# Router logits of a gated cross-attention and expert kernel: made transposed in four column groups of TensorE and turned back by a second product

## The reference

```python
x = x + tanh(g_xattn) * xattn(layernorm(x), ctx, ctx, mask, Wq, Wk, Wv, Wo, bo)
xf = layernorm(x).reshape(-1, 256)
logits = xf @ Wg + bg                      # [1024, 8], the router
idx = argmax(softmax(logits), axis=-1)     # one expert for each token
h = gelu(einsum('th,ehi->tei', xf, W1) + b1)
y = einsum('tei,eih->teh', h, W2) + b2
x = x + tanh(g_ffn) * y[t, idx[t]]
```

## Time and profile before

| What | us |
|---|---|
| median of the runs | 199.1 (lowest 198.98) |
| profiled execution | 200.14 |
| its span on the core | 198.3 |
| TensorE busy in the span | 185.5 |
| VectorE busy | 123.5 |
| ScalarE busy | 104.9 |
| GpSimd busy | 89.5 |

### The profile page before, as it was taken

One profiled execution on the slowest core, in us unless ns is written; L12 is line 12 of the kernel. 1 busy time (PEld: TensorE's weight loads), 2 busy tenths in 40 slices (PEclk: granted clock), 3 DMA queues, 4 the chain that ended last, 5 costly groups with the idle time before them and its releaser, 6 DMA issues.

```text
span 198.3 us, 4265 instructions
## 1 busy us (share of the span) xinstructions
PE 185.5 (94%) x1412; PEld 136.2 (69%) x1412; DVE 123.5 (62%) x538; ACT 104.9 (53%) x376; POOL 89.5 (45%) x128
## 2 busy tenths in 40 slices
PE   7999999999899999999999899998999999999960
PEld 6994455666665444788895666765788899989940
DVE  3479576899996421154459999997833556355520
ACT  3243438899998112211427899997631263445410
POOL 6000002577778991000003899768810024776650
PEclk9999999999999999999999999999999999999996
DMA  4998008999999990480000101600000002353011
GB/s 134 335 369 284 0 3 265 319 287 315 298 317 266 206 326 20 146 279 1 0 2 3 55 27 54 198 0 0 3 0 2 0 3 76 110 153 109 34 53 31
DMA packets 22323, 25.19 MB, mean 127 GB/s; under 512 B 1987, under 2 KB 20877, under 8 KB 22160
## 3 DMA queue, kind: packets, MB, share of 16 engines
q1 hardware_dynamic: 19536, 21.83, 37.3%
q0 software_dynamic: 1152, 2.12, 3.2%
q10 hardware_dynamic: 1600, 0.84, 1.5%
HBM read 14.14 MB, written 11.68 MB: 130 GB/s over the span
## 4 chain that ended last, share of the span: by engine, by line
PE 69%; DVE 21%; issue 3%; ACT 2%; POOL 1%; POOLq 1%; DVEq 0%
PE s_bank L1729 14%; PE o_bank L1674 14%; DVE probs L1308 12%; PE s_bank L2035 8%; PE o_bank L2046 7%; PE s_bank L1769 5%; DVE oT L1335 4%; PE s_bank L1608 3%; PE s_bank L1639 2%; PE o_bank L1817 2%; PE o_bank L1799 2%; PE t_bank L1700 2%; PE s_bank L1844 2%; ACT probs L832 2%; PE s_bank L2024 1%
## 5 line engine op out<-in xcount | busy, mean ns | idle before, releaser
L649 POOL TENSOR_TENSOR probs<-probs,r_col 128x512 f32<-128x512 f32 x32 | 33.3, 1040 | 73.8 <-DVE r_col L1319 73.7
L832 ACT ACTIVATE probs<-probs,negm_run 128x160 f32<-128x160 f32 x128 | 53.0, 415 | 6.1 <-DVE negm_run L1308 5.9
L1308 DVE CUSTOM_DVE_ANT_0 probs<-s_bank,maskneg 128x160 f32<-128x160 f32 x128 | 33.3, 317 | 3.5 <-PE s_bank L1769 3.2
L1729 PE MATMUL s_bank<-xnT,wq_sb 128*128 128x512 f32 x64 | 29.0, 600 | 0.0
L1674 PE MATMUL o_bank<-wo_sb,oT 128*128 128x256 f32 x128 | 28.7, 380 | 0.0
L1674 PEld LDWEIGHTS o_bank<-wo_sb,oT 128*128 128x128 f32 x128 | 23.9, 190 | 3.5 <-issue 0.5
L832 ACT ACTIVATION_READ_ACCUMULATOR probs<-probs,negm_run 128x1 f32 x128 | 23.9, 187 | 0.0
L1769 PE MATMUL s_bank<-k_sb,q_sb 64*128 64x160 f32 x256 | 21.7, 306 | 0.0
L1729 PEld LDWEIGHTS s_bank<-xnT,wq_sb 128*128 128x128 f32 x64 | 11.7, 190 | 13.1 <-issue 12.8
L628 POOL DMA_INDIRECT out_dram<-oT x16 | 17.0, 1064 | 7.8 <-DVE oT L1256 5.9
L1769 PEld LDWEIGHTS s_bank<-k_sb,q_sb 64*128 64x128 f32 x256 | 18.0, 187 | 2.7 <-DVE negm_run L1308 1.5
(11 more groups left out here) (169 smaller groups left out, 299.6 us busy)
## 6 DMA issues: line engine op xcount, KB each, us to landing
sorted_rows<-empty_row SPq DMA_DIRECT2D x8, 1040.0 KB, 15.6
oT<-in_L_ffn_W_dram SPq DMA_DIRECT2D x1, 2048.0 KB, 18.2
q_sb<-in_L_ffn_W_dram SPq DMA_DIRECT2D x1, 2048.0 KB, 9.4
oT<-sorted_rows SPq DMA_DIRECT2D x1, 1040.0 KB, 5.2
oT<-sorted_rows SPq DMA_DIRECT2D x8, 130.0 KB, 2.3
wq_sb<-in_L_xattn_Wq_dram SPq DMA_DIRECT2D x2, 512.0 KB, 8.1
mask_sb<-in_mask_BxSxS_bk_dram SPq DMA_DIRECT2D x2, 512.0 KB, 8.9
wv_sb<-in_L_xattn_Wv_dram SPq DMA_DIRECT2D x1, 1024.0 KB, 10.8
```

Source lines behind the costliest of these rows:

```text
L649: nc.gpsimd.tensor_tensor(window_wide(u), window_wide(u), r.rearrange("p i h -> p (i h)") .unsqueeze(2).broadcast_to([P, 4, WIDE]), ALU.mu ...
L832: last = nc.scalar.activation(window_part(u, i, h), window_part(u, i, h), ACT.Exp, bias=negm_run[at], scale=-1.0, accum_out=l_run[at])
L1308: nc.vector.tensor_tensor_reduce(window_part(u, i, h), s_bank[u % 2][:, h, i * CK:i * CK + WK], maskneg[:, q, 0:WK], -SCALE, LARGEST, ALU. ...
L1729: last = nc.tensor.matmul(bank[m % 4], wq_sb[:, c, m * P:(m + 1) * P], xnT[:, c, b * N:(b + 1) * N], start=(c == 0), stop=(c == DC - 1))
```

## The change

The weights are padded: `wg_sb` becomes [128, 2, 32] and `bg_sb` [128, 32] (`LEFT_E` = 32), zeroed by GpSimd, with 8 of the 32 columns loaded; ScalarE waits for the zeros before it issues the two loads. Now `wg_sb` is the stationary operand and the transposed tile the moving one, so a product gives logits transposed: 32 partitions (8 used) by 128 tokens. The four groups of 32 partitions of one PSUM bank hold four such products.

- Batch 0 (`batch_logits`): one group for each of the four tiles, with a bias product and two products over the contraction halves each. It is called once, after the second key product; the transposes of tile 3 move from there to after the first. VectorE copies the 128 x 128 result to `logitT` (`take_logitT`), and after the third key product TensorE transposes it back (`batch_logits_back`).
- Batch 1 (`half_logits`): two tiles per route and two contraction halves in four groups, without adding the halves. VectorE copies, and a product with `fold` (two 64 x 64 identities one over the other, made by GpSimd at the start of the attention) adds the halves and turns them back (`half_logits_back`). For route 1 the two calls stand before the projection of tile 7, with one pair of chunk transposes between them; for route 2 after the result of expert 0, with the chunk transposes of expert 4, which move up, between them.
- VectorE's `take_logitT(r)` stands at the head of `route_logits(r)` for routes 1 and 2, and after a key copy (`k1`) for route 0. `logit_ps` now counts twice per route.

The diff, cut:

```diff
+    LEFT_E = P // QT
...
+        wg_sb = sb("wg_sb", [P, DC, LEFT_E])
+        bg_sb = sb("bg_sb", [P, LEFT_E])
+        logitT = sb("logitT", [P, P])
+        fold = sb("fold", [P, DH])
...
-                sp.wait_ge(empty_ready, 2)
+                sp.wait_ge(empty_ready, 4)
...
+            nc.gpsimd.memset(wg_sb[:], 0.0).then_inc(empty_ready, 1)
+            nc.gpsimd.memset(bg_sb[:], 0.0).then_inc(empty_ready, 1)
...
             def normalise_window(b, also):
+                if b == 0:
+                    pool.wait_ge(ident_ready, E + 3)
+                    nc.gpsimd.tensor_tensor(fold[:], ident[:, 0:DH], ident[:, DH:P], ALU.add).then_inc(fold_ready, 1)
+                    pool.wait_ge(fold_ready, 1)
...
+            act.wait_ge(empty_ready, 2)
+            act.dma_start(bg_sb[:, 0:E], bg.unsqueeze(0).broadcast_to([P, E])).then_inc(s_small, 16)
+            act.dma_start(wg_sb[:, :, 0:E], wg.rearrange("(c p) e -> p c e", p=P)).then_inc(s_small, 16)
...
+            def take_logitT(r):
+                dve.wait_ge(logit_ps, 2 * r + 1)
+                nc.vector.tensor_copy(logitT[:], bank[5][:, P:2 * P]).then_inc(logitT_taken, 1)
             def route_logits(r):
...
+                logits = bank[5][:, 2 * P:2 * P + tiles * LEFT_E].rearrange("p (t e) -> p t e", e=LEFT_E)[:, :, 0:E]
+                if r > 0:
+                    take_logitT(r)
+                dve.wait_ge(logit_ps, 2 * r + 2)
...
                 if where == "k1":
+                    take_logitT(0)
                     route_logits(0)
...
+            def half_logits(r):
+                at = ROUTED[r][0]
+                pe.wait_ge(xt2_sb, at + 2)
+                part = [bank[5][g * LEFT_E:(g + 1) * LEFT_E, P:2 * P] for g in range(4)]
+                for t in range(2):
+                    nc.tensor.matmul(part[t], bg_sb[0:1, :], ones[0:1, :], start=True, stop=False)
+                for k in range(DC // 2):
+                    for g in range(4):
+                        c = g // 2 * (DC // 2) + k
+                        tt = at + g % 2
+                        last = nc.tensor.matmul(part[g], wg_sb[:, c, :], xnT[:, c, tt * P:(tt + 1) * P],
+                                                start=(g >= 2 and k == 0), stop=(k == DC // 2 - 1))
+                last.then_inc(logit_ps, 1)
+            def half_logits_back(r):
+                pe.wait_ge(logitT_taken, r + 1)
+                nc.tensor.matmul(bank[5][:, 2 * P:2 * P + 2 * LEFT_E], logitT[:], fold[:], start=True, stop=True)\
+                    .then_inc(logit_ps, 1)
+            def batch_logits():
+                pe.wait_ge(xt2_sb, QT)
+                by_tile = [bank[5][t * LEFT_E:(t + 1) * LEFT_E, P:2 * P] for t in range(QT)]
+                for t in range(QT):
+                    nc.tensor.matmul(by_tile[t], bg_sb[0:1, :], ones[0:1, :], start=True, stop=False)
                 for c in range(DC):
+                    for t in range(QT):
+                        last = nc.tensor.matmul(by_tile[t], wg_sb[:, c, :], xnT[:, c, t * P:(t + 1) * P], start=False,
+                                                stop=(c == DC - 1))
+                last.then_inc(logit_ps, 1)
+            def batch_logits_back():
+                pe.wait_ge(logitT_taken, 1)
+                nc.tensor.transpose(bank[5][:, 2 * P:3 * P], logitT[:], ident[:]).then_inc(logit_ps, 1)
...
                 if where == "k1":
-                    tile_logits(2)
+                    xn2_transposes(3)
                 elif where == "k2":
-                    xn2_transposes(3)
+                    batch_logits()
                 elif where == "k3":
-                    tile_logits(3)
+                    batch_logits_back()
...
                         project_tile(2)
-                        tile_logits(0)
                         xn2_transposes(1)
...
-                        tile_logits(1)
                         xn2_transposes(2)
...
                 xn2_transposes(QT + 1)
-                tile_logits(QT)
                 chunk_transposes(0, 2)
+                half_logits(1)
                 chunk_transposes(0, 3)
-                tile_logits(QT + 1)
+                half_logits_back(1)
                 project_tile(QT + 3)
                 ranks(1)
                 xn2_transposes(QT + 2)
                 hidden(0, 2)
-                pe.wait_ge(rank_taken, 4)
-                tile_logits(QT + 2)
                 xn2_transposes(QT + 3)
...
                 result(0, 0, expert_w2(0))
-                tile_logits(QT + 3)
+                pe.wait_ge(rank_taken, 4)
+                half_logits(2)
+                chunk_transposes(0, 4)
+                half_logits_back(2)
                 hidden(0, 3)
                 result(0, 1, expert_w2(1))
                 ranks(2)
-                chunk_transposes(0, 4)
                 result(0, 2, expert_w2(2))
```

More of the change, by code:

```diff
@@ L151, in flamingo_kernel @@
         b2_sb = sb("b2_sb", [P, E, D])
-        wg_sb = sb("wg_sb", [P, DC, E])
-        bg_sb = sb("bg_sb", [P, E])
+        wg_sb = sb("wg_sb", [P, DC, LEFT_E])
+        bg_sb = sb("bg_sb", [P, LEFT_E])
+        logitT = sb("logitT", [P, P])
         bo_sb = sb("bo_sb", [P, D])
@@ L274, in flamingo_kernel @@
         ident_ready = sem("ident_ready")
+        fold_ready = sem("fold_ready")
         pool_step = sem("pool_step")
@@ L314, in flamingo_kernel @@
         logit_ps = sem("logit_ps")
+        logitT_taken = sem("logitT_taken")
         count_ready = sem("count_ready")
@@ L783, in _ @@
             act.dma_start(bo_sb[:], bo.unsqueeze(0).broadcast_to([P, D])).then_inc(s_small, 16)
-            act.dma_start(bg_sb[:], bg.unsqueeze(0).broadcast_to([P, E])).then_inc(s_small, 16)
-            act.dma_start(wg_sb[:], wg.rearrange("(c p) e -> p c e", p=P)).then_inc(s_small, 16)
+            act.wait_ge(empty_ready, 2)
+            act.dma_start(bg_sb[:, 0:E], bg.unsqueeze(0).broadcast_to([P, E])).then_inc(s_small, 16)
+            act.dma_start(wg_sb[:, :, 0:E], wg.rearrange("(c p) e -> p c e", p=P)).then_inc(s_small, 16)
             done = act.alloc_register("act_done")
@@ L1150, in _ @@
             left = dve.alloc_register("dve_left")
+            def take_logitT(r):
+                dve.wait_ge(logit_ps, 2 * r + 1)
+                nc.vector.tensor_copy(logitT[:], bank[5][:, P:2 * P]).then_inc(logitT_taken, 1)
             def route_logits(r):
                 R = routes[r]
-                at, tiles = ROUTED[r][0] % QT, ROUTED[r][1]
+                tiles = ROUTED[r][1]
                 shape = [P, tiles, E]
-                logits = bank[5][:, at * E:(at + tiles) * E].rearrange("p (t e) -> p t e", e=E)
-                dve.wait_ge(logit_ps, r + 1)
+                logits = bank[5][:, 2 * P:2 * P + tiles * LEFT_E].rearrange("p (t e) -> p t e", e=LEFT_E)[:, :, 0:E]
+                if r > 0:
+                    take_logitT(r)
+                dve.wait_ge(logit_ps, 2 * r + 2)
                 then(nc.vector.tensor_reduce(R.lmax[:], logits, AX.X, ALU.max))
@@ L1400, in attend @@
                     nc.vector.tensor_copy(*k_dst(u + 1)).then_inc(S.k_dve, 1)
+                    also(f"k{u}")
                 dve.wait_ge(S.mask_ready, n + 1)
@@ L1442, in route_first_batch @@
             def route_first_batch(where):
-                if where == "k":
+                if where == "k1":
+                    take_logitT(0)
+                elif where == "k":
                     route_logits(0)
@@ L1686, in xn2_transposes @@
                 last.then_inc(xt2_ps, 1)
[L1688 to L1698, removed]
-                for c in range(DC):
[L1700 to L1703, removed]
+            def half_logits(r):
[11 more added lines that the diff above has]
+                last.then_inc(logit_ps, 1)
```

## The result

The changed kernel is slower: 203.13 us against 199.04, ratio 1.0219 (interval 1.0174 to 1.0264); beside other runs later it was 203.52 against 199.72, ratio 1.0172 (1.0142 to 1.0203). I had forecast 200.6, with a range up to 202.3. The profiled execution took 203.38, its span 201.6, 3.3 more than before.

A forecast was written before the change was run, and what follows sets the result against it. TensorE, busy 94% of the span, was taken to bound the kernel; -0.35 + 0.9 + 0.95 = +1.5 us turned the profiled 200.14 into 201.6, and less 1.04 for the median gave 200.6, range 198.6 to 202.3.

The forecast's parts named there:

- First batch, -0.35: Batch 0's logits: -1.0 and -0.68 from removed tiles, +1.15 batch product, +0.2 transposing back; -0.35 us, bounds -0.8 and +1.15.
- tile 1's cover of ScalarE's copy: Batch 0: tile 1's logits filled TensorE's wait for ScalarE's context copy (0.42), so removing them gains only 0.1.
- Tiles 4 and 5, +0.9: Batch 1's first pair: the return product waits for VectorE's copy behind tile 6's normalisation, delaying projection 7; +0.9, bounds 0.65 to 1.25.
- Tiles 6 and 7, +0.95: Batch 1's second pair, after result 0: halves, copy and back product 1.60 against 0.36 and 0.27 removed; +0.95, bounds +0.3 and +1.7.
- tile 6's removal gains nothing: Batch 1: tile 6's logits stood where TensorE waits for VectorE's last normalisation, so removing them only lengthens that wait.
- Sum of the logits, +1.5: Both batches' logits: -0.35 + 0.9 + 0.95 = +1.5 us.
- Rival 1: Batch product: groups run four abreast and returns are short, sum +0.15; 199.3, from 198.3 to 199.5; chance 0.22.
- Rival 2: Batch product and halves: weight loads do not overlap, 2.64 and twice 1.32; +4.0 in all, 203.1; chance 0.05.
- Rival 3: Second chunks' rows arrive late if route 2 slips over 0.95 against TensorE; slip of 2 gives 201.6 to 202.3; chance 0.07.

The follow-up runs named there:

- the copy in the pause: Kernel with only batch 1's logits changed, VectorE copying route 1's logits between tile 6's statistics and normalisation instead of after it; ratio 1.0067 to the kernel before, against 1.0085.
- the two kernels with a short jump: Changed kernel with TensorE's never-entered overflow list cut from eight chunks to four, and changed kernel with 40 never-run warming products at TensorE's head; each 200.97 us.
- 31 places in the kernel before: Kernel before, with 6 never-run warming products and a branch over them (31 instructions) at the head of TensorE's list; 201.99 us against 200.17, ratio 1.0107.
- 16 products: Changed kernel with 16 never-run warming products and a branch over them (71 instructions) at the head of TensorE's list; ratio 1.0173 to the kernel before, from two executions.
- 40 products at the head: Changed kernel with 40 never-run warming products (167 instructions) at the head of TensorE's list; 200.97 us, ratio 1.0071 to the kernel before.
- Batch 0 alone: Against the changed kernel, batch 1's logits are made tile by tile as before, only batch 0's transposed; 198.95 us against 200.17 for the kernel before, ratio 0.9955.

## Why the prediction was wrong

**The step that failed** is the sum's frame, "The profiled execution took 200.14 (span 198.3, 1.84 around it): it would be 201.6". I added the change of the chain to the span and so took everything behind the last matmul as fixed. It was not: a jump there went from 0.36 to 3.80, and TensorE's end had only 1.3 us to spare. The trace of before held the warning. The chain that I read does not end on TensorE, but on GpSimd's last scatter and its way into the rendezvous:

```profile
192.70 1.06 POOLq L137
```

TensorE's list does not end with its last matmul either, and its second jump (over the code of the other form of the kernel) took 5.1 us before and 5.3 after (4.8 to 5.5 in every kernel of this study). A jump that takes 0.36 beside one that takes 5 asks what the short one owes its shortness to. I forecast no rival of this kind, and the range ended at 202.3.

A smaller term was wrong too. I carried over the 1.04 between the profiled execution and the median of the kernel before; in the changed kernel they are 0.25 apart (203.38 and 203.13). The jump's 2.4 and this 0.8, less the 0.5 by which the second profiled execution is ahead and the 0.1 by which the logits cost less, make the 2.5 between 200.6 and 203.13.

**Point by point.**
- First batch, -0.35: measured -0.57. The mechanism holds, tile 1's cover of ScalarE's copy included; the mis-sized terms are the batch product, 0.92 instead of 1.15, and the way back, 0.11 instead of 0.2. Two slips stand in the working: by its own figures the eight bias instructions come to 0.33 + 6 x 0.037 = 0.55 and not 0.45 (0.35 measured), and the terms of the sum give -0.33.
- Tiles 4 and 5, +0.9: measured 0.93, with the copy and the signal (0.21 + 0.04) and the return product (0.43) near the 0.3 and 0.4 taken; the upper bound, 1.25, should be 1.16 by its own rows. That TensorE waits for VectorE's place in its list was shown by the copy in the pause.
- Tiles 6 and 7, +0.95: measured 1.06. That tile 6's removal gains nothing held: TensorE waits in front of tile 7's transposes for VectorE (160.84 to 161.31 in the chain), where logits stood before.
- Sum of the logits, +1.5: measured +1.42 in the stretches and +1.25 in the two kernels with a short jump (200.97 against 199.72).
- Rival 1 (four abreast) asked for a batch product under 0.8 and back products under 0.25; they took 0.92 and, in batch 1, 0.43. Rival 2 (loads don't overlap) had the number, 203.1 against 203.13 measured, by chance: its mechanism is refuted, and the batch product that it priced at 2.64 took 0.92:

```profile
98.46 0.38 PEld L1740 LDWEIGHTS t_bank<-xnT,wg_sb 128*32 128x32 f32 x16 [0.20 <-issue]
```

Sixteen loads in 0.38. The Trainium skill's page "TensorE: Matmul & The Clock Gate", Part 3, lets a load overlap a running product only in another row group; all sixteen have the same rows here, and the measurement decides. Rival 3 (late rows) did not come: from the hidden product of expert 3 to the last one it takes 26.39 (26.47 before), and the one piece of the chain there that isn't TensorE's is a copy of ScalarE of 0.38 in both (176.32; before 175.42).

**Why the jump is long.** What the runs show: its length depends on how far its target lies (8 chunks or 4) and on where both lie in the program (0, 71, 167 places further on; 14 and 16 more than before is short, 30 and 31 more is long), and not on what TensorE does. The profile's page counts the loads of program code by queue. Queue q8, whose loads come with TensorE's jumps, has in both kernels

```profile
q8 instruction: 14, 0.23, 0.6%
```

0.23 MB in 14 loads is 16 KB each. The equal count hides a difference: in the kernel before one of the 14 comes behind both jumps (196.8 to 198.3), and in the changed kernel one comes in the long jump. The view of DMA queues for its window alone, 192.0 to 195.8:

```profile
q8 instruction: 1, 0.02, 2.4%
```

Each of the four long jumps (the changed kernel twice, 31 places in the kernel before, 16 products) has one such load in its window; none of the six short ones has any. The second jump, over the other form, has two in all ten (191.6 to 196.7 before, 196.0 to 201.3 changed). With 40 products at the head one load comes ahead of the jump instead, between 185 and 192.3, where with 16 products there is none from 174 up to the jump:

```profile
q8 instruction: 1, 0.02, 1.0%
```

So in these ten profiles a jump is long when, and only when, a block of the program is loaded while it lasts. The Trainium skill, "Runtime: NRT & Kernel Launch" (Instruction fetch mechanics), says that an engine's program is fetched one after the other in blocks of 16 KB, and that a taken branch whose target lies outside the two blocks held must wait for a fetch. The trace agrees with the block size and with both lengths of the jump. That it is exactly two blocks no run here shows; nor did I try to find the exact place of the threshold.

## What to carry to other kernels

Before adding a change's cost to a span, look at which engine reaches the program's end last and with how much to spare, and at the jumps there: 30 instructions more ahead turned a jump of 0.36 us into one of 3.4 to 4.0 here, 14 or 16 did not. Measure an edit also with the program padded, or with the never-run code under a jump shortened, or its price is mixed with that of its place. A product that waits for another engine belongs behind something that engine does early: the same trick gained in batch 0, where a key product covered the copy, and lost in batch 1, where TensorE waited for the copy; that the copy stood behind a normalisation was 0.57 of the 2.0 lost. Batch 0 alone is the better kernel (0.9955).

## What the runs showed that I had not expected

A jump over code that is never run cost 2.5 us of the kernel's time (a short one against a long one in the same kernel: 200.97 and 203.52), and shifted code alone cost the kernel before 1.8. Products with one row and 32 columns run abreast as the others do: eight bias instructions in 0.35, where the old bias needed 0.33 for two.
